# A perceiver kernel on one core: context rows taken raw, key norms made among the layers, masks inside the score pieces

## The reference, cut to what matters

```python
x = x + L0_xattn(layernorm(x), ctx, itok)     # 4 decoder layers: causal attention (16 heads of 8),
                                              # cross attention to the first 32 context rows, gated FFN
x = x + L0_attn(layernorm(x))                 # 16 channels of rank 64, sigmoid messages
x = x + L0_ffn(layernorm(x))
x = x + L1_xattn(ctx, layernorm(x), mask)     # below
x = x + L1_attn(layernorm(x))                 # causal attention, 16 heads of 8
x = x + L1_ffn(layernorm(x))                  # 8 experts of width 512, the best two added

def L1_xattn(x, latents, mask, ...):          # x is the context here, latents the 64 rows
    xn = layernorm(x, ln_x_g, ln_x_b)
    ln = layernorm(latents, ln_l_g, ln_l_b)
    q = ln @ W_q                              # 2 heads of 64
    kv = concat([xn @ W_kv, ln @ W_kv], axis=1)
    qn = rmsnorm(q, q_gamma) * 64 ** -0.5
    kn = rmsnorm(k, k_gamma)
    sim = where(mask_of_keys, qn @ kn.T, -max)
    return softmax(sim) @ v @ W_out + b_out
```

## Time and profile before

| what | value |
| --- | --- |
| median of 3 runs | 498.07 us (497.87 to 498.58) |
| the profiled execution's own time | 498.65 us |
| its span, first to last instruction | 496.8 us |
| busy in the span: TensorE, VectorE, ScalarE, GpSimd | 463.5, 355.2, 275.7, 225.7 us |
| moved by DMA | 23.06 MB |
| mean granted TensorE clock | 0.986 |

### The profile page before, as it was taken

One profiled execution on the slowest core, in us unless ns is written; L12 is line 12 of the kernel. 1 busy time (PEld: TensorE's weight loads), 2 busy tenths in 40 slices (PEclk: granted clock), 3 DMA queues, 4 the chain that ended last, 5 costly groups with the idle time before them and its releaser, 6 DMA issues.

```text
span 496.8 us, 14119 instructions
## 1 busy us (share of the span) xinstructions
PE 463.5 (93%) x5346; PEld 394.1 (79%) x5365; DVE 355.2 (71%) x1053; ACT 275.7 (55%) x712; POOL 225.7 (45%) x350
## 2 busy tenths in 40 slices
PE   7998999999999999999989999987889998999996
PEld 3576777688777867899978888965879987789995
DVE  5867957667566666664598598988798986854543
ACT  3476677767686767455456365534646643533220
POOL 4352863343424232202369989776677831200000
PEclk9999999999999999999999999979898999999999
DMA  7902001010201000000330082102100000000000
GB/s 227 375 16 76 31 14 65 7 33 12 67 2 39 3 1 2 1 5 3 89 128 4 2 322 92 63 1 67 68 1 1 1 1 2 1 1 3 1 2 28
DMA packets 8988, 23.06 MB, mean 46 GB/s; under 512 B 1217, under 2 KB 4817, under 8 KB 8658
## 3 DMA queue, kind: packets, MB, share of 16 engines
q1 hardware_dynamic: 8914, 22.07, 13.0%
HBM read 21.81 MB, written 0.26 MB: 44 GB/s over the span
## 4 chain that ended last, share of the span: by engine, by line
PE 74%; DVE 10%; ACT 4%; POOL 4%; issue 4%; DMA 2%; SPq 1%; DVEq 0%; ACTq 0%; POOLq 0%
PE ps L1167 6%; PE ps L1158 6%; PE ps L1070 4%; PE ps L1082 4%; PE ps L883 4%; PE ps L873 3%; PE ps L1097 3%; PE ps L1011 3%; PE ps L942 3%; PE ps L954 3%; PE ps L975 3%; PE ps L947 3%; PE ps L865 2%; PE ps L1064 2%; PE ps L913 2%
## 5 line engine op out<-in xcount | busy, mean ns | idle before, releaser
L1680 POOL TENSOR_TENSOR rstd<-ss,par 128x1 f32<-128x1 f32 x52 | 28.5, 550 | 67.3 <-ACT sq L1187 67.1
L1735 POOL TENSOR_TENSOR rk<-rk,par 128x8 f32<-128x8 f32 (+1 forms) x32 | 46.5, 1454 | 2.7
L1215 ACT ACTIVATE own<-own 128x512 f32<-128x512 f32 x56 | 34.6, 628 | 14.2 <-DVE own L1386 9.7
L1381 DVE TENSOR_REDUCE mx<-ps 128x8 f32<-128x512 f32 x40 | 26.0, 684 | 10.2 <-PE ps L865 9.8
L1670 POOL TENSOR_TENSOR qk<-own 128x128 f32<-128x128 f32 x40 | 18.1, 455 | 32.5 <-DVE own L1374 32.2
L1070 PE MATMUL ps<-xw,xnT 128*128 128x128 f32 x208 | 30.9, 299 | 0.6 <-ACT xnT L1301 0.5
L1693 POOL TENSOR_TENSOR rstd<-mv,par 128x1 f32<-128x1 f32 x24 | 5.3, 220 | 57.1 <-DVE mv L1441 57.1
L1167 PE MATMUL ps<-we,own 128*128 128x128 f32 x256 | 30.7, 276 | 0.0
L1082 PE MATMUL ps<-own,xnT 128*128 128x128 f32 x208 | 29.5, 282 | 1.2 <-issue 0.3
L1167 PEld LDWEIGHTS ps<-we,own 128*128 128x128 f32 x256 | 29.9, 192 | 0.7 <-DVE own L1615 0.3
L1374 DVE SCALAR_TENSOR_TENSOR own<-ps,wa,trig 128x128 f32<-128x128 f32 x80 | 23.2, 341 | 9.8 <-PE ps L840 6.1
(11 more groups left out here) (247 smaller groups left out, 1307.0 us busy)
## 6 DMA issues: line engine op xcount, KB each, us to landing
cx<-ctx_in SPq DMA_DIRECT2D x8, 768.0 KB
we<-we_in SPq DMA_DIRECT2D x8, 514.0 KB, 6.5
wc<-wc_in SPq DMA_DIRECT2D x4, 768.5 KB, 5.8
wa<-wa_in SPq DMA_DIRECT2D x5, 387.0 KB, 3.0
uvT<-uvT_in SPq DMA_DIRECT2D x1, 1024.0 KB, 10.4
uv<-uv_in SPq DMA_DIRECT2D x1, 1024.0 KB, 11.0
wb<-wb_in SPq DMA_DIRECT2D x4, 128.5 KB, 4.3
wm<-wm_in SPq DMA_DIRECT2D x1, 512.0 KB, 6.1
```

The source lines that it names most:

```text
L1215: done(nc.scalar.activation(pr[:, g, a:a + 512], sd[:, g, a:a + 512], ACT.Exp), p)
L1381: done(nc.vector.tensor_reduce(mx[:, g, 8 * k:8 * k + 8].rearrange("p (r i) -> p r i", i=4), quad(od, i, g)[:, 2 * k:2 * k + 2, :, :], AX, ...
L1680: done(nc.gpsimd.tensor_tensor(rstd[:, t:t + 1], ss[:, t:t + 1], par[:, 1:2], ALU.pow), p)
L1735: done(nc.gpsimd.tensor_tensor(rk[:, n, 0:2 * w], rk[:, n, 0:2 * w], par[:, 1:2].to_broadcast([P, 2 * w]), ALU.pow), p)
```

## The change

Context rows are no longer centred and turned on the chip. A turned copy of the raw context (`keyT_in`, laid out on the host with the same values) is loaded by DMA, once for the keys (`xTe`) and once for the scores (`xT`). Mean and deviation are brought in another way: the key weights are multiplied by a centring matrix once (`w_centre`, giving `wcen`), the query likewise (second product in `qk0`/`qk1`, giving `qpc`), and what the bias of the norm adds to keys and scores, scaled by each row's deviation, is added by one bf16 product in each piece: `rowsT` holds, for each tile of 128 rows, a mask row and the deviations in three bf16 parts, and `sel`/`selq` hold the bias (`k_split`, `q_split`, `sel_q`). The scores' mask goes the same way. `c_turn` and `c_turned` are gone; `c_normed` has one pass and `c_spread` no bias, both in place in `cx`, which now has the two columns of ones and three buffers.

The key norms (`c_power`, `c_rows`, `c_keys`, `c_squares`, `c_sums`, `c_rnorm`) of all eight batches, in the order `STATS`, and their moments stand among the layers. Their rows are loaded there (`load_sample`) and, but for two batches, loaded again for `sum_ctx`.

`causal` and `cmask` are no pieces of their own. `scores` writes its mask by 16 products with 32 rows and 128 columns; `cscores` by 8, and its own products become 8 with 32 rows and 128 columns instead of 4 with 64 rows and 256. `values` is one product instead of four; its copy `vblk` is four instructions instead of two. `PLACES`, `PLACED` and `WARM` (the warming matmuls on `still`, 33 before in the table, 24 after, besides 14 at the start) are new throughout.

```diff
+STATS = (2, 3, 4, 5, 6, 7, 0, 1)
...
             elif p == "values":
                 bank = take(pe, od, p, i, g)
                 after(pe, od, "hT1", i, g)
-                for b in range(2):
-                    for a in range(2):
-                        last = nc.tensor.matmul(bank[L * a:L * a + L, L * b:L * b + L], hT[:, g, L * b:L * b + L],
-                                                wa[i % 2][:, A_V + L * a:A_V + L * a + L], start=True, stop=True)
-                done(last, p)
-            elif p == "causal":
+                done(nc.tensor.matmul(bank[:, 0:P], hT[:, g, :], wa[i % 2][:, A_V:A_V + P], start=True, stop=True), p)
+            elif p == "scores":
                 bank = take(pe, od, p, i, g)
...
-                for r in range(4):
-                    last = nc.tensor.matmul(bank[:, 512 * r:512 * r + 256], causal, it64, start=True, stop=True)
+                for c in range(2):
+                    for b in range(2):
+                        for r in range(4):
+                            rows = slice(32 * r, 32 * r + 32)
+                            late_keys = bank[L * b:L * b + L, 512 * r:512 * r + 256].rearrange("p (i k) -> p i k", k=L)[:, :, 32 * c:32 * c + 32]
+                            nc.tensor.matmul(late_keys, causal[rows, c, :], places[rows, :].rearrange("p (i k) -> p i k", k=32),
+                                             start=(c == 0), stop=True, skip_group_check=True, tile_position=(32 * r, L * b))
...
-            elif p == "cmask":
+            elif p == "cscores":
                 bank = take(pe, od, p, i, g)
...
-                for k in range(2):
-                    last = nc.tensor.matmul(bank[:, 512 * k:512 * k + 256], cmask[:, P * g:P * g + P], it32, start=True, stop=True)
...
+                for b in range(2):
+                    for r in range(4):
+                        rows = slice(32 * r, 32 * r + 32)
+                        nc.tensor.matmul(bank[L * b:L * b + L, 512 * r:512 * r + P], cmask[rows, P * g + L * b:P * g + L * b + L], places[rows, :],
+                                         start=True, stop=True, tile_position=(32 * r, L * b))
...
+                    for r in range(4):
+                        rows = slice(32 * r, 32 * r + 32)
+                        last = nc.tensor.matmul(bank[L * b:L * b + L, 512 * r:512 * r + P], qT[rows, g, L * b:L * b + L],
+                                                kcblk[rows, 2 * g + b, :, :].rearrange("p i k -> p (i k)"), start=False, stop=True,
+                                                skip_group_check=True, tile_position=(32 * r, L * b))
...
             elif p in ("qk0", "qk1"):
...
+                nc.tensor.matmul(bank[:, 0:P], xw[h0:h0 + XD, X_KT:X_KT + P], qT[h0:h0 + XD, i, :], start=True, stop=True)
+                done(nc.tensor.matmul(bank[:, P:2 * P], wcen[h0:h0 + XD, 2 * P:3 * P], qT[h0:h0 + XD, i, :], start=True, stop=True), p)
...
-                for j, c in enumerate(CG[g]):
-                    last = nc.tensor.transpose(bank[:, P * j:P * j + P], xh[i % 3][:, c, 0:D], ident)
-                done(last, p)
...
+            elif p == "c_keys":
+                bank, m = take(pe, od, p, i, g), STATS.index(i)
+                after(pe, od, "w_taken", 0)
+                after(pe, od, "k_split", 0)
+                after(pe, od, "c_rows_taken", i)
+                pe.wait_ge(s["key_loaded%d" % (m % 2)], 16 * (m // 2 + 1))
+                nc.tensor.matmul(bank[:, 0:P * width(g)], rowsT[:, i, :], sel[:, c_tiles(g), :], start=True, stop=True)
                 for j, c in enumerate(CG[g]):
...
+                    last = nc.tensor.matmul(bank[:, P * j:P * j + P], xTe[m % 2][:, P * c:P * c + P], wcen[:, 0:P], start=False, stop=True,
+                                            skip_group_check=True)
...
             elif p in ("m_tanh0", "m_tanh1"):
                 w = int(p[-1])
                 after(act, od, "m_sums%d" % (1 - w), i - 2)
+                after_all(act, od, "c_keys", STATS[-1])
+                after_all(act, od, "c_rnorm", STATS[-1])
...
             elif p == "c_sums":
                 after(dve, od, "c_squares", i, g)
-                done(nc.vector.tensor_reduce(kss[:, n, 0:2 * w], ksq[n % 2][:, 0:P * w].rearrange("p (a d) -> p a d", d=XD), AX, ALU.add), p)
+                after(dve, od, "c_power", i)
+                squares = kss[:, n, 0:2 * w]
+                step(dve, "vector_step", nc.vector.tensor_reduce(squares, ksq[:, 0:P * w].rearrange("p (a d) -> p a d", d=XD), AX, ALU.add))
+                squares = squares.rearrange("p (c h) -> p c h", h=XH)
+                done(nc.vector.tensor_tensor(squares, squares, flx[:, i, c_tiles(g)].unsqueeze(2).to_broadcast([P, w, XH]), ALU.max), p)
...
+                done(nc.gpsimd.tensor_tensor(selq[i % 2][:], cp[:, i // 2, i % 2, :].unsqueeze(1).to_broadcast([P, CT, P]), sel[:], ALU.mult), p)
...
+        def load_sample(sp, od, n):
+
+            if n >= 2:
+                after_all(sp, od, "c_moments", STATS[n - 2])
+                after_all(sp, od, "c_keys", STATS[n - 2])
+            else:
+                after(sp, od, "x_zero", n)
+            load_rows(sp, STATS[n], n % 2)
+            sp.dma_start(xTe[n % 2][:], keyT_in[STATS[n]]).then_inc(s["key_loaded%d" % (n % 2)], 16)
+
         def load_context(sp, od, b):
...
             if b >= 2:
...
+                after_all(sp, od, "c_scores", b - 2)
+            sp.dma_start(xT[b % 2][:], keyT_in[b]).then_inc(s["turned_loaded%d" % (b % 2)], 16)
+            if 1 <= b < B - 1:
+                if b == 1:
+                    after(sp, od, "x_clear", 0)
+                else:
+                    after_all(sp, od, "sum_ctx", b - 2)
+                load_rows(sp, b + 1, (b + 1) % 3)
```

More of the change, by code:

```diff
@@ L118 @@
     "m_powers": "m_power ff_sum f_power",
-    "x_turns": "l_turn q_turn c_turn top_turn u_turn o_turn",
-    "x_products": "l_qkv qk0 qk1 l_scores bwv_p c_keys c_scores top_spread sum_ctx heads o_project",
-    "x_turned": "l_turned q_turned c_turned u_turned o_turned sum_taken bwv",
+    "x_turns": "l_turn q_turn top_turn u_turn o_turn",
+    "x_products": "l_qkv qk0 qk1 l_scores w_centre w_bias q_bias c_rows c_keys c_scores top_spread sum_ctx heads o_project",
+    "x_turned": "l_turned q_turned c_rows_taken u_turned o_turned sum_taken w_taken bias_taken q_biased",
     "x_squares": "l_squares c_squares l_values qk0_taken weights",
-    "x_norms": "x_consts x_moments x_norm l_moments l_norm l_sums q_norm c_moments c_sums",
+    "x_norms": "k_split q_split x_consts x_moments x_norm l_moments l_norm l_sums q_norm c_moments c_sums",
     "x_scaled": "qk1_taken l_scaled c_scaled c_top top top_row top_diag shifted",
@@ L126 @@
     "x_powers": "x_power x_bias l_power l_rnorm x_blank x_clear c_rnorm a_power e_power",
-    "c_rows": "c_power c_normed",
+    "c_scales": "c_power c_normed sel_q",
     "e_products": "e_turn e_logits e_cho e_b2 e_up e_down",
@@ new lines @@
+    "m_turn": "3476",
+    "m_across0": "0244",
+    "m_across1": "4600",
+    "m_along0": "2244",
+    "m_along1": "4040",
+    "m_pairs0": "0422",
+    "m_pairs1": "4202",
+    "m_sums0": "6264",
+    "m_sums1": "0446",
+    "m_back": "4253",
+    "f_turn": "5600",
+    "f_mm": "0270",
+    "l_turn": "7237",
+    "l_qkv": "7237",
+    "q_turn": "2071",
+    "qk0": "4320",
+    "qk1": "5261",
+    "l_scores": "3660",
+    "w_centre": "0",
+    "w_bias": "3",
+    "q_bias": "2624",
+    "c_rows": "05120533",
@@ L1775, in load_layers @@
                 load_a(sp, l + 2)
+                if od is FAST:
+                    load_sample(sp, od, 2 * l + 2)
             if l + 2 < LAYERS:
```

903 lines of the change are left out of this document (485 added, 418 removed), and 50 rows, old and new, of the table PLACES.

## The result

The changed kernel takes 506.3 us, the median of four runs from 503.4 to 510.1. Beside it on the same chip the kernel before took 498.3 us (497.9 to 498.6). The ratio is 1.0165, with a 95% interval from 1.0097 to 1.0233. The change makes the kernel slower, and the time lies 24 us above the forecast and outside its range.

The account below looks back on a forecast made before the run. TensorE was taken to bound every stage. Layers 243.2/0.94 = 258.7 us and context 127.4/0.94 = 135.5, with 20 at the start and 66.8 at the end, gave a span of 481.0, hence 482.3 us; range 468 to 497.

Parts of the forecast that it names:

- The step that failed: Context stage, GpSimd: relieved of key powers and `c_power`, gains eight `sel_q` products of 1.5 to 4 us, falls near 50%.
- The idle share: TensorE idle taken as 6% in both layers and context stage; 4.6% would give 476.5 us, 8.1% 491.5.
- The clock: Context stage: clock stays full at 1.00, so 3.9 and 1.1 us of slow-stretch excess come off TensorE's time.
- The sum on TensorE: All instructions removed and added on TensorE: net 9.1 us less, ends -4 and 21.
- the 9 fewer: Warming matmuls on TensorE drop from 47 to 38; they run in waits, costed at nothing.
- What moved: Key norms and moments go among the layers: layers end some 27 us later, context stage some 45 us shorter.
- C: Rival, chance 0.13: layer chains queued on VectorE and GpSimd leave TensorE idle in the layers; at 14% idle, 507 us.
- D: Rival, chance 0.1: turned context rows of batches 4 to 7 queue behind expert weights, four waits of 2.5 us; 492 us.
- E: Rival, chance 0.07: nothing gained; small masks and products at upper bounds, clock still falls, 6% idle; 498.6 us.
- B: Rival, chance 0.2: larger gain, the freed order leaves almost no waits on TensorE; at 2.5% idle, 468 us.

Follow-up runs that it names:

- short maxima: Kernel with `sel_q` on VectorE, running maximum of context tiles 4 to 11 taken over 8 of 128 columns: 490.4 us, ratio 0.9828.
- repaired kernel: Changed kernel with `sel_q` moved from GpSimd to VectorE, same values: 497.0 us, ratio 0.9940 to the kernel before.
- fillers: Kernel with `sel_q` on VectorE plus 33 further warming products before eleven pieces where TensorE waited: 494.0 us, ratio 0.9881.
- all three edits: Changed kernel with `sel_q` on VectorE, `c_normed` moved from GpSimd to ScalarE, and further warming products on TensorE: 495.7 us, ratio 0.9942.

## Why the prediction was wrong

**The step that failed** is the one on GpSimd in the context stage: "`sel_q`, eight long products, comes (1.5 to 4 us each). It falls near 50%." The price was right (3.42 us), and the share came out lower still (58.70 of 150, 39%). What wasn't asked is whom an instruction of 3.4 us on GpSimd keeps from working. It was costed by GpSimd's own share, as if engines only met at semaphores. In its place the runs showed a stall of VectorE, of up to 3 us for one instruction, that cost 9 to 11 us in all: 506.3 and 508.2 against 497.0. In the two profiled runs 10.7 us of the difference lie behind the layers, where `sel_q` runs. That is less than half of the 24 us. All of it shows up in the next two terms, idle share and clock, which also hold the rest.

**The idle share**, 6% in both stretches, was right in the layers (17.3 of 260, 6.7%) and wrong behind them (14.5%). The text itself put VectorE near 86% there and then took less idle time than the earlier trace rows had for that load. Even with `sel_q` repaired, 10.2% were left. The short maxima show the size of what was passed over: 0.4 to 0.8 us for each us of VectorE. By that rate the 8.0 us of `sel_q` on VectorE are 3 to 6 us of the 15 between 497.0 and 482.3, an estimate from these runs.

**The clock**, taken as 1.00 without a reason from the rows, was 0.97, 0.91 and 0.98, the 20.2 us of the split above. In the repaired kernel the fillers were worth 2 to 3 us, 4 with the short maxima in place, and 0.6 with `c_normed` on ScalarE. They had been costed at nothing in the prediction ("they run in waits"), and the 9 fewer were not asked about; a table of fillers placed for one order of work covers the waits of that order.

**The sum on TensorE** held: 9.1 us less were forecast, with ends of -4 and 21. The windows give 17.0 in the changed kernel and 13.1 in the one with `sel_q` on VectorE, a little of it records that are missing (5653 matmuls beside 5681 weight loads on the page). By the start distances the masks were priced too high: `causal` was to gain 2 us, where 20 times 0.3 are some 6, though the run of it alone gave 1.7; `cscores` was to take 10.4 us, where 16 times some 0.47 are 7.5, a gain of 6.9 and not 4.

**What moved** was right in size. The layers ended 31.6 us later (last `y3` 242.5 and 274.1), forecast 27. VectorE was at 205.3 us from 20 to 280, forecast 205, and GpSimd at 147.7, forecast 160 (its terms add to 171 before the halving of `kc`, which has no price there). But what follows the layers became 20 us shorter and not 45; 31 with `sel_q` on VectorE.

**The rivals.** C had the right sign and, by luck, nearly the right time (507; its terms add to 506), and the wrong place: it needed 14% idle in the layers, behind GpSimd's and VectorE's queues. The idle time there is 6.7%, no wait names GpSimd, and the powers and moments taken away gave at most 3 to 5 us and nothing. D: no wait of TensorE names a DMA. E had the falling clock right, but the masks were cheap. B: 486.4 is the best that was seen, with 4.4% idle, a clock of 0.99 and the maxima over fewer columns. No rival had the mechanism that decided.

**Open**: why the clock among the layers was 0.97 in the changed kernel and 0.99 or 1.00 in others with the same instructions up to the first `sel_q` at 288 us. It moves the end of the layers by 3 to 6 us (274.1 and 276.1 against 269.7 to 271.2 in the kernels that keep `c_normed` on GpSimd, but for 272.0 with short maxima alone). Two profiles of the changed kernel show it, none of the others, and no run was made for it; a single profile of each kernel can't tell a property of the kernel from chance. Also open is what a `sel_q` cut into parts is worth, and what stalls of 1.1 us cost.

## What to carry to other kernels

A long GpSimd instruction with its operands in SBUF is costed twice: on its own engine, and as a stall until it ends for a VectorE instruction of two kinds that was seen to stand: with two operands in SBUF, or an SBUF tile with a per-row scalar. Here VectorE could do it in 1.0 us where GpSimd took 3.4, and it belonged there, even with VectorE the busier engine; whether cutting it up on GpSimd helps was not shown. And where a forecast makes TensorE's work denser beside an engine at 85%, that engine's time has a price: take some from it before promising the denser stage, and set the warming products anew for the new order.

## What the runs showed of the hardware

- A VectorE maximum of two SBUF tiles took 3.44 us in place of 0.42 under a GpSimd product, and a subtraction of a PSUM tile (L1641, 128x512), at 358.88 us beside another, kept its 0.69.
- The product of 128x1664 bf16 took 3.42 us on GpSimd and 1.02 us on VectorE.
- bf16 products of 32 rows by 128 columns in small tiles started 8 ns apart (16 in 0.13 us) before products of the same tiling and 15 ns (16 in 0.24) before others, where 17 ns was the smallest distance that the trace of before had shown.
- The runs of one program differ with the granted clock: the ten of the changed kernel lie between 503.4 and 512.7 us, and its first four have a clock of 0.956, 0.971, 0.977 and 0.965 for 510.1, 506.4, 503.4 and 506.2 us. With fillers the spread was smaller: 12 runs with all three edits lie within 3.8 us, 12 without the fillers (`c_normed` on ScalarE) within 9.3.
